# The diagonal blocks of the second scores: masked by VectorE in PSUM instead of by TensorE

## The reference, cut to what matters

```
scores = einsum('bqhd,bkhd->bhqk', q, k) * scale          # 16 heads of 16
scores = where(pos_k <= pos_q, scores + slope * (pos_k - pos_q), -1e9)
attn = softmax(scores)
out = einsum('bhqk,bkhd->bqhd', attn, v) @ out_w.T + out_b
```

## Time and profile before

| | us |
|---|---|
| median of 3 runs | 888.2 (885.59 to 892.02) |
| the profiled execution | 886.07 |
| its span in the trace | 884.1 |
| busy: PE, DVE, ACT | 770.2, 593.3, 490.6 |
| first and last second-stream product | 217.8, 865.9 |

### The profile page before, as it was taken

One profiled execution on the slowest core, in us unless ns is written; L12 is line 12 of the kernel. 1 busy time (PEld: TensorE's weight loads), 2 busy tenths in 40 slices (PEclk: granted clock), 3 DMA queues, 4 the chain that ended last, 5 costly groups with the idle time before them and its releaser, 6 DMA issues.

```text
span 884.1 us, 13585 instructions
## 1 busy us (share of the span) xinstructions
PE 770.2 (87%) x4841; PEld 368.6 (42%) x4846; DVE 593.3 (67%) x1214; ACT 490.6 (55%) x1007; POOL 158.7 (18%) x296
## 2 busy tenths in 40 slices
PE   3577789776799999999999999999999999879895
PEld 1244355321244454445444444544444453223343
DVE  5999885596566766676677667666765766778122
ACT  2266748740466565655565555556555655546562
POOL 1323340046400000000000000000000003660112
PEclk9788899875799999999999999999999999999998
DMA  9801225544330352353236223622642221240011
GB/s 298 262 19 56 81 79 166 182 148 151 114 83 1 111 128 83 75 117 112 67 75 124 82 67 100 130 77 83 111 125 67 72 84 49 74 170 12 13 37 48
DMA packets 78439, 86.97 MB, mean 98 GB/s; under 512 B 34729, under 2 KB 61852, under 8 KB 77980
## 3 DMA queue, kind: packets, MB, share of 16 engines
q1 hardware_dynamic: 72418, 74.84, 30.4%
q0 software_dynamic: 3328, 9.38, 3.5%
q10 hardware_dynamic: 2626, 1.89, 0.8%
HBM read 40.34 MB, written 28.32 MB: 78 GB/s over the span
## 4 chain that ended last, share of the span: by engine, by line
PE 66%; DVE 13%; ACT 7%; issue 6%; DMA 2%; POOL 2%; SPq 1%; ACTq 1%; another core or an unknown queue 1%; POOLq 0%; DVEq 0%
PE bank L1519 15%; PE bank L1497 12%; PE bank L1477 12%; PE bank L1445 8%; PE bank L1455 5%; PE bank L1534 4%; DVE PM L1211 2%; ACT PR L801 2%; PE bank L1312 2%; PE bank L1355 2%; PE bank L1560 2%; ACT U L790 2%; DVE ACC L855 1%; DMA qk_parts<-TG 1%; PE bank L1480 1%
## 5 line engine op out<-in xcount | busy, mean ns | idle before, releaser
L1211 DVE TENSOR_REDUCE PM<-bank 128x1 f32<-128x512 f32 (+3 forms) x640 | 364.7, 605 | 181.7 <-PE bank L1480 130.5
L801 ACT ACTIVATE PR<-bank 128x512 f32<-128x512 f32 (+3 forms) x640 | 327.9, 534 | 279.4 <-PE bank L1497 144.6
L1497 PE MATMUL bank<-OPS 111*128 111x512 bf16 (+3 forms) x640 | 224.3, 354 | 27.5 <-ACT PR L801 18.1
L1477 PE MATMUL bank<-OPS 108*128 108x512 bf16 (+3 forms) x640 | 231.4, 367 | 10.4 <-issue 5.7
L1519 PE MATMUL bank<-PR,VS 128*17 128x512 f32 (+3 forms) x1280 | 157.5, 544 | 2.5 <-ACT PR L801 0.4
L1497 PEld LDWEIGHTS bank<-OPS 111*128 111x128 bf16 x640 | 62.4, 98 | 107.0 <-ACT PR L801 75.7
L1477 PEld LDWEIGHTS bank<-OPS 108*128 108x128 bf16 x640 | 64.3, 101 | 97.6 <-DVE PM L1211 56.9
L528 POOL TENSOR_TENSOR NP<-NM,NIL 128x8 bf16<-128x8 f32 x32 | 7.6, 239 | 497.9 <-DVE NM L1219 497.8
L1445 PE MATMUL bank<-WB 128*128 128x256 f16 x552 | 91.0, 273 | 1.0
L1445 PEld LDWEIGHTS bank<-WB 128*128 128x128 f16 x552 | 47.8, 100 | 42.2 <-issue 21.2
L1480 PE MATMUL bank<-MASK 128*128 128x128 bf16 x256 | 58.6, 229 | 0.0
(11 more groups left out here) (177 smaller groups left out, 807.9 us busy)
## 6 DMA issues: line engine op xcount, KB each, us to landing
WB<-W SPq DMA_DIRECT2D x23, 512.0 KB, 3.6
x_rows<-PR SPq DMA_DIRECT2D x23, 256.0 KB, 3.2
WB<-in_w SPq DMA_DIRECT2D x23, 256.0 KB, 3.4
y_rows<-XT SPq DMA_DIRECT2D x23, 256.0 KB, 3.1
OPS<-qk_parts SPq DMA_DIRECT2D x28, 192.0 KB
OPS<-qk_parts SPq DMA_DIRECT2D x28, 128.0 KB
W<-in_w SPq DMA_DIRECT2D x6, 512.0 KB, 5.6
qk_parts<-WB SPq DMA_DIRECT2D x8, 384.0 KB, 3.8
```

The costliest lines, as they stand in the source:

```text
L801: act.activation(PR[:, tile % RING, off:CH], PS[2 + tile % 2][:, off:CH], ACT.Exp).then_inc(b_exped, 1)
L1211: dve.tensor_reduce(PM[:, c % 2, j, xq, gg:gg + 1], bank[:, 0:width], AX.X, ALU.max).then_inc(a_reduced, 1)
L1477: last = mm(bank[:, 0:width], OPS[0:ROWS_A, h % 4, 0, P * (TC * a + xq):P * (TC * a + xq) + P], OPS[0:ROWS_A, h % 4, 1, CH * gg:CH * gg + ...
L1497: last = mm(bank[:, off:CH], OPS[0:ROWS_B, h % 4, 1, P * k:P * k + P], OPS[0:ROWS_B, h % 4, 0, CH * b + off:CH * b + CH], start=True, stop ...
```

## The change

For the 256 diagonal tiles of the second stream the product with the triangle is gone from PE. Instead VectorE replaces the first 128 columns of the tile, in the bank, by their minimum with a table (-2^30 above the diagonal, 2^127 elsewhere; the table takes the place of the old triangle in `MASK`). ScalarE's exponential of such a tile waits for the new semaphore `b_masked` instead of `b_scored`. VectorE's instruction stands in its list right behind the reduction (and row maxima) of the same step.

```diff
+DIAGONAL = [tile for tile in range(TOTAL) if diagonal(tile)]
...
 def exponential(tile):
-                act.wait_ge(b_scored, tile + 1)
+                if tile in DIAGONAL:
+                    act.wait_ge(b_masked, DIAGONAL.index(tile) + 1)
+                else:
+                    act.wait_ge(b_scored, tile + 1)
...
+            def mask_b(tile):
+
+                _, c, _, k = place_b(tile)
+                off = P * (k - TC * ORDER[c])
+                block = PS[2 + tile % 2][:, off:off + P]
+                dve.wait_ge(b_scored, tile + 1)
+                if tile == 0:
+                    dve.wait_ge(cast_in, 32)
+                dve.tensor_tensor(block, block, MASK[:, 1, :], ALU.min).then_inc(b_masked, 1)
...
                     if ended is not None:
                         row_maxima(ended)
+                if n - LEAD in DIAGONAL:
+                    mask_b(n - LEAD)
...
                 last = mm(bank[:, off:CH], OPS[0:ROWS_B, h % 4, 1, P * k:P * k + P],
-                          OPS[0:ROWS_B, h % 4, 0, CH * b + off:CH * b + CH], start=True, stop=k < TC * b)
-                if k >= TC * b:
-                    last = mm(bank[:, off:off + P], MASK[:, 1, :], MASK[:, 2, :], start=False, stop=True)
+                          OPS[0:ROWS_B, h % 4, 0, CH * b + off:CH * b + CH], start=True, stop=True)
                 last.then_inc(b_scored, 1)
...
-                      np.where(q < k, far, 0.0),
+                      np.where(q > k, far, 2.0 ** 127),
```

More of the change, by code:

```diff
@@ L81, in place_b, with diagonal @@
     return p, c, k // 2, 2 * g + k % 2
+def diagonal(tile):
+    _, c, _, k = place_b(tile)
+    return k >= TC * ORDER[c]
 TURN_AT = {chunk_end(m) - 1 + (17, 17, 11, 5)[m] if m < NC else chunk_end(m) - 1 + 5: m for m in range(NC * PAIRS)}
@@ L277, in build @@
             sem("row_max"), sem("max_part"), sem("mt_ps"), sem("mt_copied"), sem("b_scored"))
-        b_exped, pv_done, u_ready, o_ps, o_rc = (
-            sem("b_exped"), sem("pv_done"), sem("u_ready"), sem("o_ps"), sem("o_rc"))
+        b_exped, b_masked, pv_done, u_ready, o_ps, o_rc = (
+            sem("b_exped"), sem("b_masked"), sem("pv_done"), sem("u_ready"), sem("o_ps"), sem("o_rc"))
         o_normed, up_ps, glu_done, gate_th, gate_read = (
```

## The result

| | before | after |
|---|---|---|
| median, us | 888.7 (885.6 to 892.0, 4 runs) | 949.6 (942.9 to 954.6, 4 runs) |
| ratio, 95% interval | | 1.067 (1.0625 to 1.0714) |
| the profiled execution: span | 884.1 | 947.8 |
| busy: PE, DVE, ACT | 770.2, 593.3, 490.6 | 775.2, 643.8, 494.9 |

933 was forecast, in a range of 902 to 954. The sign and the mechanism came out as forecast; the size was 14 us too low in the medians (+61 in place of +47).

The account below looks back on a forecast made before the run. PE was taken as fullest but in lockstep with VectorE and ScalarE. Delays of 32 (five middle pairs), 4 (first), 6 (seventh) and 5 us (last), saved products included, added 47 to 886.1: 933 us, range 902 to 954.

Parts of the forecast that it names:

- What bounds: Whole kernel: PE is fullest, busy 87% of the span, but its two streams run in lockstep with VectorE and ScalarE.
- Part 1: PE: 256 removed mask products at 0.058 us each would gain 14.8 us at best, if PE never waited for the mask.
- Part 2: VectorE: each mask takes 0.28 us until usable and 0.21 us of engine time, judged by the division of the heads.
- Part 3: Diagonal runs: masks wait behind VectorE's reductions, delaying exponentials and products; chunks 0 to 3 lengthen by 2.0, 2.0, 1.0, 1.4 us.
- five of eight: Diagonal runs: five of each run's eight masks have their length on the path; used to size a dearer mask.
- The sum: All pairs: five middle pairs add 32 us, the first 4, the seventh 6, the last 5; 47 in all.
- rival D: PE's clock falls in one run of each pair, about 2 us each time, 16 us more: 949 us; chance 0.03.
- A: Diagonal runs: masks find VectorE free and PE gains its 14.8 us: 871 us; chance 0.05.
- B: Diagonal runs: only the mask's latency, no queue behind reductions; 0.65 us a run, 21 us in all: 907 us; chance 0.20.
- C: VectorE: the mask is dearer, 0.40 us instead of 0.28, 19 us more: 952 us; chance 0.07.
- Signals: Trace signs listed beforehand: mask length, waits for masks, run and pair lengths, clock, and PE's loads waiting for exponentials.

Follow-up runs that it names:

- product and minimum: The change with the product with the old triangle put back on PE, so each diagonal tile is masked twice: 950.5 us, ratio 1.068 to before.
- the repeated run: The change itself, unaltered, timed again on another chip against the kernel before: 954.2 us, ratio 1.071.
- the kernel with ratio 0.999: The change with the minimum after the exponential, in SBUF, one step late, ahead of the reduction (also "the early minimum"); scores scaled down: 889.9 us against 889.8 before.
- the spare minimum: Kernel before without masks, VectorE doing 240 like minima on first-stream banks into spare SBUF, nothing of the second stream waiting: 869.9 us, ratio 1.000.

## Why the prediction was right, and where its size was off

**What bounds.** Right: PE was the fullest engine but in lockstep with the others. Taking its products away altogether brought 6.2 us.

**Part 1.** The best case of 14.8 us was more than twice what there is (measured 6.2). It stood in the sum only through the runs.

**Part 2.** 0.28 us for the mask, measured 0.288; 0.21 us of VectorE's time, measured 0.20 (510.27 to 510.47 in the timeline). The nearest row was the right one. The estimate from the Trainium skill, 0.26 us of engine time ("VectorE: DVE Perf Modes", the section on the TRN2 errata), is not what this trace shows.

**Part 3.** The step-by-step working held to 0.11 us in the run that it followed, and for a pair it gave 87.8 us where 88.2 was measured. That is in part luck: the four runs grew by 2.2, 1.7, 0.9 and 1.3 us (forecast 2.0, 2.0, 1.0 and 1.4), 6.1 in all and not 6.4, and the tiles between them by 0.7, where nothing was forecast. That "five of eight" masks have their length on the path was too many: 3 to 4.

**The sum.** This is the step that was mis-sized. By the two profiles the parts took: pairs 2 to 6 +40.4 us (forecast 32), the first +3.9 (4), the seventh +5.0 (6), the last +5.6 (5), the end +1.5 (0), and the start up to the first second-stream product +7.3 (0): 63.7. Two terms make up most of the difference:

- Falls of the clock. 5 x 6.8 = 34 of the 40.4 would be there with the clock up; 6.4 are four falls in three of the five pairs, 1.6 us each. I had this as rival D at 0.03, one fall a pair, 2 us each and 16 us in all. It happened beside my forecast and not in its place, and the sign that the clock would stay at 1.00 between 254 and 700 us failed. I had bounded it by PE's longest single wait, 0.9 us, and taken that as too short. One of the falls:

```profile
402.40 0.23 PE L1519 MATMUL bank<-OPS 111*128 111x128 bf16 x1 [0.95 <-ACT PR L811]
402.46 0.38 PE L1499 MATMUL bank<-OPS 108*128 108x512 bf16 x1
403.45 0.39 PE L1519 MATMUL bank<-OPS 111*128 111x256 bf16 x1 [0.60 <-POOL VS L527]
403.94 0.29 PE L1534 MATMUL bank<-ONEB,ZERO 128*128 128x128 bf16 x1
404.16 1.91 PE L1539 MATMUL bank<-PR,VS 128*17 128x512 f32 x8
```

The value products of 404.16 take 1.91 us where the same ones take 1.05 at the full clock. From the pair's first product (397.52) to the fall no wait of PE is longer than 0.95 us. At the same place of the kernel with product and minimum that wait is 0.89 and the clock stayed up, so the longest wait does not tell the two apart.

- The start. Its 7.3 us lie ahead of the first mask. In the repeated run the distance from the first product of the first stream to the first of the second is 33.5 us, 3.1 more than in the profile of before, and in the kernel with ratio 0.999 on the same chip it is 33.6. What causes it was not tried.

The repeat shows that this split is one of several. Against the kernel with ratio 0.999 on its chip (spans of 953.9 and 886.9 us) the start has only +1.0, pairs 2 to 6 again +40.9, but the first pair +9.0, the seventh +8.5 and the last with the end +7.8, with more time at half clock in all three (23.5, 17.1 and 25.8 us against 15.6, 13.7 and 8.7). The five middle pairs are the firm part; my 4, 6 and 5 for the others came close in the first profile and not in the second.

**Rivals.** A fell: masks do not find VectorE free. B, 907, has the right two ingredients, but the kernel with the mask ahead of the reduction (ratio 1.031, or 916) shows what is left without that queue. C fell at 0.288 us. D came true in kind, with four falls in three middle pairs and 6.4 us; that its 949 us is almost the median is luck.

**Signals.** The exponentials waited 172.9 us for the mask, more than the 121 for the product. The masks themselves hardly waited: eight in ten started 0.2 to 1.3 us after the modelled end of their product (0.3 to 0.9 was forecast). PE's loads waited 81 us more, where 40 was forecast. The non-diagonal tiles of a pair grew by 0.7 us in all and gave nothing back.

## What to carry to other kernels

An instruction moved to a less busy engine costs what its place in that engine's list costs: look when the engine comes to it and how many banks or buffers lie between it and whoever waits, not at its idle share. With two banks in turn, a delay at the reader reaches the writer two tiles later; walking one repeated stretch of the trace through, with start-to-start distances, gave that delay here to 6% for a pair and to 15% for a single run. And where a busy TensorE loses work and gains short waits, allow for its clock: here it took 6.4 of the 40.4 us of the middle pairs.

## What the runs showed of the hardware

- VectorE's minimum of 128 columns takes 288 ns in a PSUM bank and 286 ns in SBUF; with 16 columns in the bank 175 ns. From these two widths one gets 1.0 ns a column and, as an estimate, 0.16 us that do not depend on them. The next instruction starts 0.20 us after one of 128 columns (510.27 and 510.47 in the timeline above).
- The granted clock of TensorE fell from 2.4 to 1.2 GHz in six of ten middle pairs of the change, eight times in all. In the run of diagonal tiles in which it fell, PE's longest wait before the fall was 0.95 us in six cases and 1.2 us in the two others; in the kernel with the mask ahead of the reduction it fell three times behind waits of at most 0.78 us. With the products put back beside the minimum it did not fall in five of five pairs.
- The same kernel took 870 us on two chips and 890 on a third. No kernel was profiled on both kinds, but two that match the kernel before in time were: the spare minimum (870 us) and the early minimum (890 us). Their middle pairs are alike (81.8 and 81.3 us). The first product of the second stream came 24.7 and 33.6 us behind that of the first stream, the first pair took 69.9 and 76.9 us, the seventh 75.6 and 83.0. So the difference lies ahead of the second stream and in the first and seventh pairs.
